# An attention stage with its products taken later by VectorE, seven banks at the start, and projections in halves

## The reference

```
attention (32 heads of 16, causal) -> ffn (1792, low-rank scaled weights) -> mamba-like scan -> ffn (1376)

q, k, v = x @ Wq.T + bq, x @ Wk.T + bk, x @ Wv.T + bv
scores  = where(causal, q @ k.T / sqrt(16), -inf)
out     = softmax(scores) @ v
out     = out @ Wo.T + bo
```

## Time and profile before

| | |
|---|---|
| median of 3 runs | 4375.56 us (4364.9 to 4380.09) |
| the profiled execution | 4379.33 us |
| its span, first to last instruction | 4377.6 us |
| TensorE busy | 3945.8 us (90%) |
| VectorE busy | 2830.3 us (65%) |
| ScalarE busy | 1451.3 us (33%) |
| GpSimd busy | 1938.0 us (44%) |
| granted TensorE clock, mean | 0.906 |

### The profile page before, as it was taken

How to read it: one execution, slowest core, us unless ns; L and a number is a source line. 1 busy time by engine, 2 the same in 40 slices (tenths; PEclk the granted TensorE clock), 3 DMA queues, 4 the chain that set the end, 5 groups by cost and what they waited for, 6 DMA issues and landing times.

```text
span 4377.6 us, 60652 instructions
## 1 busy us (share of the span) xinstructions
PE 3945.8 (90%) x18308; PEld 2848.3 (65%) x18308; DVE 2830.3 (65%) x5290; ACT 1451.3 (33%) x2386; POOL 1938.0 (44%) x1951
## 2 busy tenths in 40 slices
PE   7889799779999999979778997997899999999797
PEld 4444477567777777757654444775577777777576
DVE  3567344578888888864435573445688888888644
ACT  1344311244433444431113344112444334443311
POOL 1111332356666666654311113323566666666543
PEclk8787699899999999989976778998899999999899
DMA  3221011011001110001132210110110001100011
GB/s 71 35 41 33 20 44 36 19 37 32 25 24 29 34 31 29 22 15 45 40 71 35 35 31 28 44 36 19 37 32 25 24 29 34 31 26 24 15 45 40
DMA packets 80972, 145.11 MB, mean 33 GB/s; under 512 B 16152, under 2 KB 18056, under 8 KB 80784
## 3 DMA queue, kind: packets, MB, share of 16 engines
q1 hardware_dynamic: 80784, 142.84, 12.6%
HBM read 112.64 MB, written 4.19 MB: 27 GB/s over the span
## 4 chain that ended last, share of the span: by engine, by line
PE 66%; issue 11%; DVE 10%; POOL 5%; ACT 3%; DVEq 2%; POOLq 1%; SPq 1%; DMA 0%; ACTq 0%
PE banks L486 14%; PE banks L487 13%; PE banks L488 13%; PE banks L666 4%; PE banks L827 4%; PE banks L647 3%; PE banks L623 3%; DVE conv L1328 3%; PE banks L838 2%; PE banks L820 2%; PE banks L530 2%; POOL wg_lo L1593 1%; ACT conv L998 1%; POOL X L1498 1%; DVEq L1331 1%
## 5 line engine op out<-in xcount | busy, mean ns | idle before, releaser
L1328 DVE SCALAR_TENSOR_TENSOR conv<-banks,cpar,conv 128x509 f32<-128x509 f32 (+2 forms) x576 | 428.1, 744 | 89.4 <-ACT conv L998 75.1
L1156 DVE TENSOR_TENSOR Y<-banks,Y 128x512 f32<-128x512 f32 x400 | 275.6, 692 | 233.5 <-PE banks L488 233.3
L941 ACT ACTIVATE probs<-banks 128x1024 f32<-128x1024 f32 (+3 forms) x384 | 298.3, 809 | 309.2 <-PE banks L647 308.4
L1568 POOL TENSOR_SCALAR_AFFINE_SELECT probs<-probs 128x256 f32<-128x256 f32 x256 | 103.9, 406 | 656.4 <-ACT probs L941 656.0
L623 PE MATMUL banks<-stack_k,stack_q 48*128 48x512 f32 (+3 forms) x768 | 327.1, 495 | 61.6 <-DVEq L1202 19.6
L1479 POOL TENSOR_SCALAR f_hi<-f_raw 128x512 fp32r<-128x512 f32 x150 | 93.5, 623 | 581.9 <-PE banks L488 473.0
L486 PE MATMUL banks<-xhi,f_hi 128*128 128x512 f32 x800 | 328.5, 411 | 3.5 <-DVE xlo L1127 3.5
L486 PE MATMUL banks<-xhi,wx_hi 128*128 128x512 f32 x768 | 312.6, 407 | 16.3 <-DVE conv L1328 16.3
L487 PE MATMUL banks<-xhi,f_lo 128*128 128x512 f32 x800 | 319.8, 400 | 0.0
L488 PE MATMUL banks<-xlo,f_hi 128*128 128x512 f32 x800 | 319.5, 399 | 0.0
L487 PE MATMUL banks<-xhi,wx_lo 128*128 128x512 f32 x768 | 306.3, 399 | 0.0
(11 more groups left out here) (203 smaller groups left out, 10205.7 us busy)
## 6 DMA issues: line engine op xcount, KB each, us to landing
m_raw<-in_w_mamba SPq DMA_DIRECT2D x224, 256.0 KB, 2.7
f_raw<-in_w_ffn SPq DMA_DIRECT2D x50, 768.0 KB, 4.6
stack_q<-part_hi SPq DMA_DIRECT2D x128, 64.0 KB, 2.4
stack_k<-part_hi SPq DMA_DIRECT2D x128, 64.0 KB, 2.5
X<-in_x SPq DMA_DIRECT2D x4, 1024.0 KB, 6.5
wqk_raw<-in_w_attn SPq DMA_DIRECT2D x8, 512.0 KB, 3.6
stack_q<-part_lo SPq DMA_DIRECT2D x64, 64.0 KB, 2.4
stack_k<-part_lo SPq DMA_DIRECT2D x64, 64.0 KB, 2.5
```

The costliest lines, as they stand in the source:

```text
L941: act.activation(probs[n % 2][:, 2 * p:2 * p + 2, 0:w], banks[:, 2 * p:2 * p + 2, 0:w], ACT.Exp, scale=1.0 / HD ** 0.5).then_inc(exp_done[ ...
L1156: dve.tensor_tensor(Y[:, i, :], bank[6 + i % 2], Y[:, i, :], ALU.add).then_inc(f["dn_used"], 1)
L1328: r = dve.scalar_tensor_tensor(out=rest, in0=src[:, 0:HALF - lag], scalar=cpar[:, o:o + 1], in1=rest, op0=ALU.mult, op1=ALU.add)
```

## The change

- **Lag.** Each shared use of a bank is now two or more entries: proj has two halves of 6 matmuls, proj_hi (ACT) and proj_lo (VectorE); values_in is followed later by values_out, maxima by maxima_out, turn by turn_out. VectorE and ACT do their part at the later entry, some pieces behind TensorE.
- **Banks by table.** `ring_banks` walks the list once and gives each use the allowed bank whose last user is released earliest; TensorE waits for that release (ring_free, part_lo_ready or mt_ready), and the drains after part_lo and mt_lo are gone. Up to the first score seven banks are allowed, then 4, 5 and 7.
- **Order.** Only 2 values tiles come before the pieces of quad 0 and 2 among them; the last 4 follow steps 0 to 3 of quad 0, their values_out one step later. In quads 1 and 3 the halves of the projections follow steps 0, 1, 3, 4, 6, 7, 9, 10, with proj_lo in steps 2, 5, 8, 11. Turns follow steps 2 and 8, and turn_out comes in steps 3 and 9.
- **Stacks.** A semaphore for each of the 4 heads of each parity, so that pieces of a head wait for its 6 DMAs.
- **SP.** Weights 1 are loaded ahead of stacks 0 and 1 (the bias tile has two slots for that); put_maxima 0 and weights 2 come ahead of the wait for v_used.

```diff
             for use in range(4):
-                yield "proj", 0, use
-            for i in range(5):
+                yield from project(0, use)
+            for i in range(2):
                 yield "values_in", i
+                yield "values_out", i
             for n in range(NP):
-                if n in (3, 9, 15):
-                    yield "values_in", 5 + (n - 3) // 6
-                if n in (21, 27, 33, 39):
-                    yield "proj", 1, (n - 21) // 6
-                yield "piece", 0, n
+                if n in (6, 12):
+                    yield "values_in", 1 + n // 6
+                if n in (8, 14):
+                    yield "values_out", 1 + n // 6
+                if n >= 18 and n % 6 == 0 and n < 42:
+                    yield "proj", 1, n // 6 - 3, 0
+                if n >= 18 and n % 6 == 3 and n < 42:
+                    yield "proj", 1, n // 6 - 3, 1
+                    yield "proj_hi", 1, n // 6 - 3
+                if n >= 24 and n % 6 == 0:
+                    yield "proj_lo", 1, n // 6 - 4
+                yield from some(1)
             yield "maxima", 0
+            yield from some(2)
+            yield "maxima_out", 0
+            yield from some(AHEAD - 2)
...
+                        if n == NS - 2 and q == 2 and t + 1 < NQ:
+                            yield "maxima_out", t + 1
+                        if q == 1 and n == 3 and t > 0:
+                            yield "turn_out", t - 1, 1
+                        if q == 1 and n == 9:
+                            yield "turn_out", t, 0
+                        if q == 1 and t == 0 and 0 < n < 5:
+                            yield "values_out", n + 3
+                        if q == 0 and t in (1, 3) and n in (2, 5, 8, 11):
+                            yield "proj_lo", (t + 3) // 2, n // 3
                     if n > 0:
                         yield "values", t, n - 1
-                    if n == 1 and t > 0:
+                    if t == 0 and n < 4:
+                        yield "values_in", n + 4
+                    if n == 2 and t > 0:
                         yield "turn", t - 1, 1
-                    if n == 7:
+                    if n == 8:
                         yield "turn", t, 0
-                    if t % 2 and n < 8 and n % 2 and (t + 3) // 2 < NQ // 2:
-                        yield "proj", (t + 3) // 2, n // 2
+                    if t in (1, 3) and n % 3 < 2:
+                        yield "proj", (t + 3) // 2, n // 3, n % 3
+                    if t in (1, 3) and n % 3 == 1:
+                        yield "proj_hi", (t + 3) // 2, n // 3
...
+        def ring_banks():
+
+            last, bank_of, before = {}, {}, {}
+            for use in RING_USES:
+                started_at = ORDER.index(use)
+                main = started_at >= ORDER.index(("score", 0, 0, 0))
+                allowed = MAIN_BANKS if main else FIRST_BANKS
+                k = min(allowed, key=lambda i: (last[i][2] if i in last else -1))
+                bank_of[use[:3]], before[use[:3]] = k, last.get(k)
+                last[k] = release(use)
+                if not main:
+                    first_scores = dict(last)
+            return bank_of, before, first_scores
...
                 ones_in(0)
+                load_qk(1)
                 stack(0)
                 stack(1)
-                load_qk(1)
+                put_maxima(0)
+                load_qk(2)
                 held(sp, v_used, b + 1)
                 ones_in(1)
-                put_maxima(0)
-                load_qk(2)
                 stack(2)
                 stack(3)
...
-                        if n == 0:
-                            pe.wait_ge(stacked[t % 2], (b * (NQ // 2) + t // 2 + 1) * STACKED)
-                        pe.wait_ge(ring_free, b * RING + ring - 2)
+                        if i == 0:
+                            pe.wait_ge(stacked[t % 2][h], (b * (NQ // 2) + t // 2 + 1) * STACKED)
+                        bank_free(BEFORE[use])
...
                         if use == 0 and f > 0:
-                            act.wait_ge(stacked[0], (b * (NQ // 2) + f) * STACKED)
-                            act.wait_ge(stacked[1], (b * (NQ // 2) + f) * STACKED)
+                            for par in range(2):
+                                for h in range(QUAD):
+                                    act.wait_ge(stacked[par][h], (b * (NQ // 2) + f) * STACKED)
```

More of the change, by code:

```diff
@@ L211, in build @@
         part_hi_ready, part_lo_ready = sem("part_hi_ready"), sem("part_lo_ready")
-        stacked = [sem("stacked0"), sem("stacked1")]
+        stacked = [[sem(f"stacked{par}_{h}") for h in range(QUAD)] for par in range(2)]
         ones_rows = sem("ones_rows")
@@ L299, in attention_order @@
                         yield "score", t, n, q
-                        turning = n == NS - 2 and q < 2 and t + 1 < NQ
                         if n == NS - 2 and q == 1 and t + 1 < NQ:
                             yield "maxima", t + 1
-                        for _ in range(0 if turning else 2 if n in (2, 3) and q == 0 else 1):
-                            if pieces:
-                                yield "piece", *pieces.pop(0)
+                        turning = n == NS - 2 and q < 2 and t + 1 < NQ
@@ new lines, in attention_order @@
+                        yield from some(0 if turning else 2 if n in (2, 3) and q == 0 else 1)
+                        if n == NS - 2 and q == 2 and t + 1 < NQ:
[6 more added lines that the diff above has]
+                            yield "values_out", n + 3
@@ L318, in build, with release @@
         ORDER = list(attention_order())
+        RING_USES = [o for o in ORDER if o[0] in ("piece", "values_in", "maxima", "turn") or o[0] == "proj" and o[3] == 0]
+        RING_ENDS = [o[:3] for o in ORDER if o[0] in ("piece", "values_in", "maxima", "turn") or o[0] == "proj" and o[3]]
+        RING = len(RING_ENDS)
+        FREED = {"piece": "piece", "values_in": "values_out", "turn": "turn_out"}
+        FREES = [o for o in ORDER if o[0] in FREED.values()]
+        FREE = len(FREES)
+        def release(use):
+            kind, *arg = use
+            if kind == "proj":
+                return "part_lo_ready", 4 * arg[0] + arg[1] + 1, ORDER.index(("proj_lo", *arg[:2]))
+            if kind == "maxima":
+                return "mt_ready", arg[0] + 1, ORDER.index(("maxima_out", *arg))
+            end = (FREED[kind], *arg)
+            return "ring_free", FREES.index(end) + 1, ORDER.index(end)
@@ L364, in stack @@
                                 sp.dma_start(dst[at:at + HD, h, :].bitcast(F32),
-                                             part[src, which, :].bitcast(F32)).then_inc(stacked[par], 16)
+                                             part[src, which, :].bitcast(F32)).then_inc(stacked[par][h], 16)
                 def put_maxima(t):
@@ L924, in _ @@
                         if use == 0 and f > 0:
[L925 to L932 removed]
+                            for par in range(2):
+                                for h in range(QUAD):
+                                    act.wait_ge(stacked[par][h], (b * (NQ // 2) + f) * STACKED)
+                        act.wait_ge(ring_done, b * RING + RING_ENDS.index(("proj", f, use)) + 1)
+                        act.activation(part_hi[:, which, s * HALF:(s + 1) * HALF], bank[RING_BANK["proj", f, use]],
+                                       ACT.Identity, bias=qk_b[:, f % 2, which:which + 1]).then_inc(part_hi_ready, 1)
                     elif what == "score" and arg[2] % 2:
```

150 lines of the change are left out of this document (70 added, 80 removed).

## The result

The changed kernel takes 4394.85 us (median of 12 runs, 4384.49 to 4399.74) against 4375.42 for the kernel before in the same runs: a ratio of 1.0039, 95% interval [1.0026, 1.0052]. It is slower by 17 us (0.4%), where 54 us of gain were forecast, and the interval excludes a ratio of 1. The profiled execution took 4395.95 us, with a span of 4394.2.

A forecast was written before the change was run, and what follows sets the result against it. TensorE was taken to bound the quads, slowed by half clock and stalls, and latency the first stage. Terms -62.8, +43.3, -26.2 and -8 sum to -53.7: 4379.3 profiled becomes 4325.6, named 4322 for the median; range 4280 to 4366.

The forecast's parts named there:

- first stage: Up to the first score: earlier pieces and stacks bring that score to 99 us; -62.8 us over both batches.
- the new wait at quad 1: TensorE stands still about 13 us on stack_q<-mt_lo, as put_maxima(1) stands behind 48 stack copies in SP's queue.
- quad 0: Four values tiles moved in and a new wait in SP's queue: 61 us instead of 40.7 and 38.0, +43.3 us.
- quads 1 and 3: Quads with projections: halves remove most VectorE waits for ACT, POOL's split adds a wait; 55 and 54 us, -26.2 in all.
- quads 2, 4, 5, 6: Turns taken later, drains gone, banks held for 2 to 6 pieces: 1 us gained a quad, -8 us.
- quad 7: Last quad of each batch, which has no pieces: 0 us.
- Then a wait of 14 us stays: First stage: part_hi of the second projection waits until all 48 stack copies have landed, at 76.9 us.
- 99 + 9.5 + 11.2 + 2.3 + 1.6 = 123.6: Time of v_used in quad 0: first score, steps 0 to 3, four tiles, first tile's half clock, half a step and drain.
- 2 for banks: Quads 1 and 3: 2 us of waits for banks, counted in the 55 us for quad 1.
- Rival D: Pieces on two banks: 160 pieces each pay one more 0.43 us wait, 69 us, giving 4391; 8%.
- C: Gain eaten: values tiles and steps 0 to 3 at half clock (28 us), halves gain nothing (26); 4376, 12%.
- the rule against the rows: The skill says activity releases TensorE's throttle; the prediction objected that profile rows show full busyness at a 0.50 clock.

The follow-up runs named there:

- e1: The changed kernel with put_maxima(1) moved between stack(2) and stack(3) in SP's list: 4366.59 us, ratio 0.9998 to the kernel before.
- e2: The changed kernel with all last six values tiles in the first stage and none in quad 0's steps: 4345.6 us, ratio 0.9951 to the kernel before.
- e7: e5 with whole projections behind steps 1, 3, 5 and 7 of quads 1 and 3, VectorE's part a step later: 4321.0 us, ratio 0.9874.
- e8: e5 with turns as in e6 and whole projections, part_hi and part_lo at once: 4299.25 us, ratio 0.9829 to the kernel before.
- e9: e5 with turns still behind steps 2 and 8, but taken by VectorE at once: 4305.44 us, ratio 0.9834 to the kernel before.
- e6: e5 with turns behind steps 1 and 7 and taken by VectorE at once, as in the kernel before: 4302.67 us, ratio 0.9836.
- e5: The changed kernel with the edits of e2 and e3 together: 4317.49 us, ratio 0.9877 to the kernel before.
- e4: The changed kernel with turns back behind steps 1 and 7, turn_out still a step later: 4393.35 us, ratio 1.0042 to the kernel before.
- e11: e8 with two banks (4 and 5) instead of three behind the first score: 4477.03 us, ratio 1.0216 to the kernel before.
- e3: The changed kernel with POOL's weight split for projections 2 and 3 at step 5 of quads 0 and 2: 4388.18 us, ratio 1.0041 to the kernel before.

## Why the prediction was wrong

It named the mechanism that gave the first stage's gain back, and priced it well: the new wait at quad 1 was forecast at 13 us near 150 and came as 12.62 us at 158.7. The signs that it named came true as well: the first score at 103.9 us, two waits on mt_lo (12.6 and 14.5 us), and 5.1 us for wqk_lo twice a batch. None of the signs against it did, for 61.5 us of bank waits over the 330 pieces of batch 0 are 0.19 us a piece. Yet the sign of the sum was wrong, because all five stages were missed on the same side. By the sum's own terms, both batches, forecast and measured in the profiled executions:

| term | forecast | measured |
|---|---|---|
| first stage | -62.8 | -51.0 |
| quad 0 | +43.3 | +55.5 |
| quads 1 and 3 | -26.2 | -9.4 |
| quads 2, 4, 5, 6 | -8 | +12.2 |
| quad 7 | 0 | +11.8 |
| rest | 0 | -2.5 |
| sum | -53.7 | +16.6 |

**First stage: right up to the last piece, then mis-sized.** "Then a wait of 14 us stays" stands in the rows: TensorE does its last pieces meanwhile and stands idle for 9.38 us until part_lo at 77.73, of 14 us in which it is busy 4.62. "Last piece near 94.7" came too: the last one ended on TensorE at 98.61 - 3.73 = 94.88. But the 4.4 us to the first score count from VectorE's folding of the maxima (125.11 in the earlier trace rows), and VectorE was still working off the filled banks. Its folding, and the rest of the chain:

```profile
98.31 0.17 DVE L1298 TENSOR_TENSOR mx<-mx 128x16 f32<-128x16 f32 x1
...
100.27 0.27 DVE L1304 TENSOR_SCALAR mt_hi<-banks 32x128 fp32r<-32x128 f32 x1
```

So TensorE stood idle for 3.73 us. From the folding to the first score it was 5.6 us and not 4.4, since the list now has two pieces of quad 1 ahead of maxima_out, and VectorE took them first: 1.66 us from the transpose at 98.61 to mt_hi, 0.55 in the kernel before. The first score came at 103.9, not 99. Pieces ahead of VectorE and a later maxima_out are the change's own lag, here on the path.

**Quad 0: the step that was mis-sized is v_used**, "99 + 9.5 + 11.2 + 2.3 + 1.6 = 123.6". SP went on at 134.4, when VectorE's drain had ended. Of these 10.8 us, 4.9 are the later first score. From the first score it was 30.5 us instead of 24.6. The four tiles took 5.1, 3.0, 4.3 and 3.0 us to the next score matmul, 15.4 for 13.5: the granted clock was 0.50 until 110.8, nearly all of the first tile, and again until 124.5, the larger part of the third. Step 4 began at 132.22, so steps 0 to 3 without the tiles took 28.3 - 15.4 = 12.9 us against "I take 9.5"; that is nearer to the 14.2 at half clock of the earlier trace rows, though the mean clock of the stretch was 0.83. 2.8 us of it are idle time. Half of step 4 and the drain took 2.2 for 1.6. The 2.5 + 30.3 + 2.8 = 35.6 us from there on were nearly right (171.33 - 134.40 = 36.9). e1 and e2 confirm the chain, the first by taking 15 us a batch out of it, the second by taking all of it.

**Quads 1 and 3: the split's wait and the clock were right, "2 for banks" was not.** POOL's split held TensorE for 5.1 us, twice a batch, against a forecast of 5.1 to 5.3. Half-clock time was 55.7 us over the four quads for "some 12" each. But TensorE was idle for 10.2 to 10.9 us in each of these quads where 5.3 + 2 were counted, so 5 to 6 us went to other waits than the split's. That is 12.9 us of the 16.8 that this term was off. "Its waits mostly go" failed with it: before, with 4.5 us of waits for the split in batch 0 and 3.5 in batch 1, all idle time was 7.2 to 9.2 us a quad, so the other waits, at 5.9 us a quad, were hardly longer than now. And e7 and e8 show no difference between halves and whole projections. The term's other end, halves that bring nothing (26 us more, so 0), is nearer to the -9.4 than the value taken.

**Quads 2, 4, 5, 6: the step that failed by its sign.** "Turns are taken a step later by VectorE [...] each turn, values tile or projection now holds one of three banks for 2 to 6 pieces. I take 1 us a quad gained." The text names the cost and then counts a gain. Measured: 0.9 us more of idle time a quad ((21.8 - 14.5) / 8) and 12 us longer in all. e9 and e6 against e5, and e8 against e7, put the lag at 19, 18 and 20 us in the two batches, by the ratios, each good to 12 to 16 us; over some 30 turns that is about half a microsecond a turn. e4 shows that the place alone isn't it.

**Rival D** gave 4391, close to the 4394.85 measured, but not for its reason. It priced 160 pieces at 0.43 us. Taking the third bank away altogether costs 0.26 us a piece (e11), so pieces that had two banks only now and then cost at most 42 us, and the lag's experiments give about half of that. The rest of the miss lies in the first stage and quad 0, where D said nothing. C asked for 28 us more of quad 0 and nothing from the halves, and gave 4376: nearest in kind, since quad 0 did cost 12 more and the halves did bring nothing.

**Quad 7** was counted at 0, because it has no pieces. It was 11.8 us longer, by its clock (0.54 for 0.94 in batch 1). The turns' place changes there too, and by the table it goes with the length of quad 7 in 13 of 14 kernels; so the term was left out without a reason, and whether the place is the cause stays open. e4, with the old place, has 71.3 us and still the changed kernel's time.

Three smaller readings of the prediction don't hold. A mean clock of 0.63 to 0.85 means 1.2 GHz for 30 to 74% of the time, not "a third to a half". The 23.9 us of waits for VectorE's reduces are the plain ones alone, 40.6 with the masked. And the chain of quad 0 gives 159.2 - 99 = 60.2 us, which was rounded up to 61.

On **the rule against the rows**, the trace was the better guide. In e11 TensorE is busy 52.35 of 54.70 us of a quad and gets 0.50 all the while. The Trainium skill ("TensorE: Matmul & The Clock Gate", section "What's actually happening") has activity releasing the throttle; by busy time alone, this run does not agree.

The 70 us between forecast and result are five terms of 12 to 20 us each. Idle time and half-clock time part them: in quads 1 and 3 the miss is mostly waits, in quad 7 it is the clock alone, and in quads 2, 4, 5 and 6 it is 7 us of idle time and 12 us more at half clock, which are worth 6.

## What to carry to other kernels

When work that frees a buffer is moved later, look at the queue that fills the buffer: whatever stands behind the bulk in that queue moves with it. Here a transfer of two rows waited behind 48 copies of 0.63 us, and four tiles moved out of a stage that had 9.4 us of idle TensorE gave the whole gain of that stage back; leaving them there kept it.

A result taken later holds its buffer for longer. With three banks, and a piece behind every score, that cost about half a microsecond a turn, and a lag of the maxima put 1.1 us on the path to the first score. Seven banks instead of three brought 16 us in the first stage; the lag of that stage was not tried without them. Size a change's parts apart: the new first stage with all values tiles in it, the table of banks and an early split of the weights are together worth 75 us here, while four tiles moved out (38), a split behind step 0 (32) and the lag of the turns (about 20) lost 92.

## What the runs showed of the hardware that was not expected

- A bank fewer can cost a multiple of its waits through TensorE's clock. With two banks instead of three, TensorE's idle time over the eight quads without projections was 19 us (13 with three), but its half-clock time rose from 147 to 412 us. A TensorE that was busy 96% of quad 2 got 1.2 GHz for all of it.
- Less idle time can come with more half-clock time: in e3 quad 1 lost 7 us of idle time and got 4 us longer (0.82 to 0.66), and in e6 9 us less idle time over eight quads came with 23 us more at half clock. Each is a single execution.
- A stretch with the same instructions can take 40% longer by its clock, even within one execution: quad 7 of the kernel before took 42.0 us at 0.51 in batch 0 and 29.5 at 0.94 in batch 1.
